# First attention: V of a group projected beside its own pairs, two places for transposed x, weight units by halves of the columns

## What is computed

```python
Q = jnp.einsum('bqd,hde->bqhe', x, W_Q) + b_Q
K = jnp.einsum('bkd,hde->bkhe', x, W_K) + b_K
V = jnp.einsum('bkd,hde->bkhe', x, W_V) + b_V
scores = jnp.einsum('bqhe,bkhe->bhqk', Q, K) / np.sqrt(d_head)
A = jax.nn.softmax(jnp.where(causal, IGNORE, scores), axis=-1)
z = jnp.einsum('bhqk,bkhe->bqhe', A, V)
x = _layernorm(x + jnp.einsum('bqhe,hed->bqd', z, W_O) + b_O)
```

## Time and profile before

| | us |
|---|---|
| median of three executions | 1614.74 |
| their spread | 1612.95 to 1619.67 |
| the profiled execution, its time | 1618.39 |
| its span, first to last instruction | 1616.6 |
| PE busy in the span | 1541.5 (95%) |
| DVE busy | 998.3 (62%) |
| ACT busy | 687.4 (43%) |
| POOL busy | 187.6 (12%) |

### The profile page before, as it was taken

One profiled execution on the slowest core, in us unless ns is written; L12 is line 12 of the kernel. 1 busy time (PEld: TensorE's weight loads), 2 busy tenths in 40 slices (PEclk: granted clock), 3 DMA queues, 4 the chain that ended last, 5 costly groups with the idle time before them and its releaser, 6 DMA issues.

```text
span 1616.6 us, 28670 instructions
## 1 busy us (share of the span) xinstructions
PE 1541.5 (95%) x11112; PEld 1330.8 (82%) x11112; DVE 998.3 (62%) x2113; ACT 687.4 (43%) x1809; POOL 187.6 (12%) x207
## 2 busy tenths in 40 slices
PE   6999999899999999989999899999989899999997
PEld 5888888689899999978888677777767798989896
DVE  6777776845454545575666567788864554444446
ACT  0544544622222222212233277788873344444443
POOL 1222222310000000020000114122210000000001
PEclk9999999999999999989999999999998899999999
DMA  6000100001010101100000376678740000000101
GB/s 209 2 15 1 41 2 1 27 25 40 22 43 27 50 26 38 32 1 33 1 33 1 44 124 86 87 100 135 95 66 27 1 26 27 27 26 14 38 0 52
DMA packets 43065, 66.51 MB, mean 41 GB/s; under 512 B 4560, under 2 KB 33488, under 8 KB 42832
## 3 DMA queue, kind: packets, MB, share of 16 engines
q1 hardware_dynamic: 42960, 65.09, 19.9%
HBM read 36.24 MB, written 2.10 MB: 24 GB/s over the span
## 4 chain that ended last, share of the span: by engine, by line
PE 86%; DVE 8%; DMA 2%; issue 2%; ACT 2%; SPq 1%; POOL 1%; DVEq 0%; POOLq 0%; ACTq 0%
PE ps L83 22%; PE ps L84 21%; PE ps L85 21%; PE ps L1617 3%; PE ps L1631 2%; PE ps L370 2%; PE ps L394 2%; PE ps L1662 2%; PE ps L1607 2%; PE ps L381 2%; PE ps L1645 1%; DMA nQs<-nQc_h 1%; PE ps L364 1%; PE ps L1604 1%; SPq L1459 1%
## 5 line engine op out<-in xcount | busy, mean ns | idle before, releaser
L880 DVE TENSOR_TENSOR m6hT_l<-m6h,m6hT_h 128x512 fp32r<-128x512 f32 x128 | 88.4, 692 | 185.5 <-ACT m6hT_h L785 185.4
L787 ACT ACTIVATE m2hT_h<-ps 128x512 fp32r<-128x512 f32 x128 | 76.4, 597 | 287.3 <-PE ps L85 287.3
L882 DVE SCALAR_TENSOR_TENSOR m2hT_l<-ps,m2hT_h 128x512 fp32r<-128x512 f32 x128 | 88.4, 691 | 162.0 <-ACT m2hT_h L787 161.9
L784 ACT ACTIVATE m6h<-ps,m6b 128x512 f32<-128x512 f32 x128 | 88.0, 688 | 216.2 <-PE ps L85 201.6
L1731 ACT ACTIVATE nPr<-ps,negm 128x128 f32<-128x128 f32 x512 | 146.7, 383 | 23.3 <-DVE negm L1828 23.3
L83 PE MATMUL ps<-w_h,m6hT_h 128*128 128x256 f32 x512 | 145.3, 284 | 2.4 <-DVE X L918 1.8
L85 PE MATMUL ps<-w_h,m6hT_l 128*128 128x256 f32 x512 | 145.7, 285 | 0.0
L84 PE MATMUL ps<-w_l,m6hT_h 128*128 128x256 f32 x512 | 145.0, 283 | 0.0
L85 PE MATMUL ps<-m2w_h,m2hT_l 128*128 128x256 f32 x448 | 126.8, 283 | 0.0
L84 PE MATMUL ps<-m2w_l,m2hT_h 128*128 128x256 f32 x448 | 126.7, 283 | 0.0
L83 PE MATMUL ps<-m2w_h,m2hT_h 128*128 128x256 f32 x448 | 126.3, 282 | 0.0
(11 more groups left out here) (286 smaller groups left out, 4310.6 us busy)
## 6 DMA issues: line engine op xcount, KB each, us to landing
nKm<-nKc_h SPq DMA_DIRECT2D x64, 128.0 KB, 4.6
nQs<-nQc_h SPq DMA_DIRECT2D x64, 128.0 KB, 5.9
raw<-in_w_e1i SPq DMA_DIRECT2D x9, 512.0 KB, 3.3
raw<-in_w_e1o SPq DMA_DIRECT2D x9, 512.0 KB, 3.2
raw<-in_w_e6i SPq DMA_DIRECT2D x9, 512.0 KB, 3.3
raw<-in_w_e6o SPq DMA_DIRECT2D x9, 512.0 KB, 3.4
raw<-in_w_a SPq DMA_DIRECT2D x8, 512.0 KB, 4.4
nKm<-nKc_l SPq DMA_DIRECT2D x32, 128.0 KB, 5.4
```

Of the source, the lines that this page charges most:

```text
L784: nc.scalar.activation(c.h32[:, u % 2, :], ps[:, u % 2, :], ACT.Gelu, bias=bias)
L787: nc.scalar.activation(c.hT[0][:, ch, :], ps[:, u % 2, :], ACT.Relu).then_inc(c.s["hi_ready"], 1)
L880: last = nc.vector.tensor_tensor(c.hT[1][:, ch, :], c.h32[:, u % 2, :], c.hT[0][:, ch, :].bitcast(F32), ALU.subtract)
L882: last = nc.vector.scalar_tensor_tensor(c.hT[1][:, ch, :], ps[:, u % 2, :], 0.0, c.hT[0][:, ch, :].bitcast(F32), ALU.max, ALU.subtract)
```

## The change

V of a group is projected in the first two steps of its own pairs (V0 behind T0 and V1 behind T1 of step 4G, V2 and V3 in step 4G+1) and no longer before them. The places of the next group's fills move: x to step 4G, Q0 and Q1 to step 4G+1, Q2 and Q3 to 4G+2, K0 to K3 to 4G+3, K3 behind the values. The transposed x has two places, since V of a group still reads its own while that of the next is written. The weight units hold one half of the columns for both chunks, so the first two fills of Q need one unit. The high halves of units 1 to 5 are written by ACT, the low ones by DVE. DVE copies x low ahead of the low half of unit 0, and the wait for the row and V bias loads moves to K2's place. The constants of the mixtures move a little, the columns' load stands one place earlier, and the transposes of the mixture's x begin at step 30.

```diff
+    def w_of_step(p):
+
+        G, k = divmod(p, 4)
+        if G >= NGW:
+            return [[], [], [], []]
+        own, later = [("v", (G, j)) for j in range(4)], G + 1 < NGW
+        q, key = ([(kind, (G + 1, j)) for j in range(4)] if later else [] for kind in "qk")
+        return ([own[0:1], own[1:2], [("x", (G + 1, 0))] if later else [], []],
+                [own[2:3], own[3:4], q[0:1], q[1:2]],
+                [q[2:3], q[3:4], [], []],
+                [key[0:1], key[1:2], key[2:3], key[3:4]])[k]
+
+    def w_start():
+        return [("x", (0, 0))] + [(kind, (0, j)) for kind in "qk" for j in range(4)]
+
+    w_place = {f: F for F, f in enumerate(w_start() + [f for p in range(NP) for at in w_of_step(p) for f in at])}
...
-    def w_fills(G):
-        return [(kind, (G, j)) for kind in "qkv" for j in range(4)] + ([("x", (G + 1, 0))] if G + 1 < NGW else [])
-
-    def w_of_step(p):
-
-        G, k = divmod(p, 4)
-        return w_fills(G + 1)[3 * k:3 * k + (4 if k == 3 else 3)] if G + 1 < NGW else []
...
-    W_X_AT, W_U_AT, W_W_AT = 28, NP, (28, 30)
+    A1_BY_ACT = (1, 2, 3, 4, 5)
+    W_X_AT, W_U_AT, W_W_AT = 30, NP, (28, 30)
...
-            w, unit = (w_q, 2) if kind == "q" else (w_k, 4)
-            if G == 0 and j == 0:
-                pe.wait_ge(prep_done, U_A1 + unit)
+            w, unit = (w_q, 0) if kind == "q" else (w_k, 2)
+            xh, xl = W.XT[G % 2]
+            if G == 0 and j % 2 == 0:
+                pe.wait_ge(prep_done, U_A1 + (unit + 1 + j // 2))
...
-            if G == 0 and j == 0:
...
+            if G == 0 and b == 0:
+                pe.wait_ge(prep_done, U_A1 + (5 + half))
...
-                pe.wait_ge(consts_dve, 7)
+                pe.wait_ge(consts_dve, 2)
...
-        x_hi(1)
+        for k in A1_BY_ACT:
+            act.wait_ge(raw_loaded[k % 2], (U_A1 + (k - k % 2)) * 8 + 16)
+            nc.scalar.activation(wA1[0][:, k * RAW:(k + 1) * RAW], raw[k % 2][:, :], ACT.Identity).then_inc(split_act, 1)
...
+            if kind == "x":
+                split_first()
+                w_vector_start(v)
+            elif (kind, i) in extra:
...
+            sp.dma_start(cols[:, :], cols_in).then_inc(cols_loaded, 16)
             load_a1(1)
-            sp.dma_start(cols[:, :], cols_in).then_inc(small_loaded, 16)
...
-            split_a1(0)
-            split_a1(1)
-            v.wait_ge(small_loaded, 48)
-            w_vector_start(v)
...
+            def high_a1():
+
+                v.wait_ge(raw_loaded[0], 16)
+                nc.vector.tensor_scalar(wA1[0][:, 0:RAW], raw[0][:, :], 1.0, None, ALU.mult).then_inc(split_hi, 1)
+
+            def low_first():
+                v.wait_ge(split_hi, 1)
+                nc.vector.tensor_tensor(wA1[1][:, 0:RAW], raw[0][:, :], wA1[0][:, 0:RAW].bitcast(F32), ALU.subtract).then_inc(prep_done, 1)
+
+            def low_a1(k):
+
+                v.wait_ge(split_act, A1_BY_ACT.index(k) + 1)
+                v.sem_inc(split_hi, 1)
+                w = cut(wA1, k * RAW, RAW)
+                nc.vector.tensor_tensor(w[1], raw[k % 2][:, :], w[0].bitcast(F32), ALU.subtract).then_inc(prep_done, 1)
+
+            def last_low():
+                low_a1(5)
+                v.wait_ge(small_loaded, 32)
+
+            nc.vector.memset(mhalf[:, :], -0.5).then_inc(consts_dve, 1)
+            v.wait_ge(consts_pool, 7)
+            nc.vector.tensor_copy(identb[:, :], ident[:, :]).then_inc(consts_dve, 1)
             mix_vector_start(v, M2)
             m2 = mix_vector_parts(v, M2)
-            w_vector(v, link, {("q", (0, 0)): lambda: split_a1(2), ("q", (0, 1)): lambda: split_a1(3), ("q", (0, 2)): constants,
-                               ("q", (0, 3)): lambda: split_a1(4), ("k", (0, 0)): lambda: split_a1(5),
-                               ("k", (0, 2)): lambda: split_a1(6), ("v", (0, 0)): lambda: split_a1(7)}, M2, m2)
+            high_a1()
+            w_vector(v, link, lambda: (low_first(), low_a1(1)),
+                     {("q", (0, 0)): lambda: low_a1(2), ("q", (0, 2)): lambda: low_a1(3), ("q", (0, 3)): constants,
+                      ("k", (0, 1)): lambda: low_a1(4), ("k", (0, 2)): last_low,
+                      ("v", (0, 1)): lambda: split_a1(6), ("v", (0, 3)): lambda: split_a1(7)}, M2, m2)
...
+    def halved(c):
+        return c.reshape(128, 2, 2, 512).transpose(0, 2, 1, 3).reshape(128, -1)
...
-    x["w_a1"] = np.concatenate([chunked(heads(a[f"L0_attn_W_{n}"])) for n in "QKV"]
+    x["w_a1"] = np.concatenate([halved(chunked(heads(a[f"L0_attn_W_{n}"]))) for n in "QKV"]
```

More of the change, by code:

```diff
@@ L164, in program @@
     consts_dve = sem("consts_dve")
+    cols_loaded = sem("cols_loaded")
     small_loaded = sem("small_loaded")
@@ L170, in program @@
     split_hi = sem("split_hi")
+    split_act = sem("split_act")
     split_whole = sem("split_whole")
@@ L208, in program @@
     GW, WT, NGW, NP = 2, 2 * S, B // 2, 2 * B
-    WF = 13
     W = Stage()
@@ L219, in program @@
     w_slot(0)
-    W.XT = pair(m, "wXT", [P, DC, WT])
+    W.XT = [pair(m, "wXT0", [P, DC, WT]), None]
     W.V[0] = m.place("wV0", [P, GW, H, 64], F32)
@@ L232, in program @@
     W.bq8 = m.place("wbq8", [P, 8], F32)
+    W.XT[1] = pair(m, "wXT1", [P, DC, WT])
     W.s = signals("w", "g_full xt_hi g_evac bq_ready s_full s_max p_exp rec_done p_ready pt_full pt_ready z_full zt_hi zt_ready "
@@ L235, in program @@
     W.ctx_loaded = [sem("w_ctx_loaded0"), sem("w_ctx_loaded1")]
-    w_q, w_k, w_v = ([t[:, i * 2048:(i + 1) * 2048].rearrange("p (k n) -> p k n", k=DC) for t in wA1] for i in range(3))
+    w_q, w_k, w_v = ([t[:, i * 2048:(i + 1) * 2048].rearrange("p (h k n) -> p h k n", h=2, k=DC) for t in wA1] for i in range(3))
     w_o = [t[:, 3 * 2048:4 * 2048].rearrange("p (k n) -> p k n", k=8) for t in wA1]
@@ L239, in program, with w_fill @@
     G0 = 4
-    def w_fill(G, kind, j=0):
-        return WF * G + {"x": 0, "q": 1, "k": 5, "v": 9}[kind] + j
-    def w_fills(G):
-        return [(kind, (G, j)) for kind in "qkv" for j in range(4)] + ([("x", (G + 1, 0))] if G + 1 < NGW else [])
     def w_of_step(p):
         G, k = divmod(p, 4)
-        return w_fills(G + 1)[3 * k:3 * k + (4 if k == 3 else 3)] if G + 1 < NGW else []
+        if G >= NGW:
[9 more added lines that the diff above has]
+    w_place = {f: F for F, f in enumerate(w_start() + [f for p in range(NP) for at in w_of_step(p) for f in at])}
+    def w_fill(G, kind, j=0):
+        return w_place[kind, (G, j)]
     def w_pairs(*at):
@@ L328, in project @@
                 for i in range(DC):
-                    last = split3(nc, bank[:, c2 * WT:(c2 + 1) * WT], w[0][:, i, ch * P:(ch + 1) * P],
-                                  w[1][:, i, ch * P:(ch + 1) * P], W.XT[0][:, i, :], W.XT[1][:, i, :], i == 0, i == DC - 1)
+                    wh, wl = (t[:, ch // 4, i, ch % 4 * P:(ch % 4 + 1) * P] for t in w)
+                    last = split3(nc, bank[:, c2 * WT:(c2 + 1) * WT], wh, wl, xh[:, i, :], xl[:, i, :], i == 0, i == DC - 1)
             last.then_inc(s["g_full"], 1)
         def project_v(G, j):
-            if G == 0 and j == 0:
-                pe.wait_ge(prep_done, U_A1 + 6)
+            b, half = divmod(j, 2)
+            xh, xl = W.XT[G % 2]
+            if G == 0 and b == 0:
+                pe.wait_ge(prep_done, U_A1 + (5 + half))
             bank = g_fill(w_fill(G, "v", j))
-            b, half = divmod(j, 2)
-            cols_v = slice(half * GT, (half + 1) * GT)
             for i in range(DC):
-                last = split3(nc, bank, W.XT[0][:, i, b * S:(b + 1) * S], W.XT[1][:, i, b * S:(b + 1) * S],
-                              w_v[0][:, i, cols_v], w_v[1][:, i, cols_v], i == 0, i == DC - 1)
+                last = split3(nc, bank, xh[:, i, b * S:(b + 1) * S], xl[:, i, b * S:(b + 1) * S],
+                              w_v[0][:, half, i, :], w_v[1][:, half, i, :], i == 0, i == DC - 1)
             last.then_inc(s["g_full"], 1)
@@ L419, in w_tensor @@
                     transpose_p(2 * (p - 2) + half)
-                for kind, i in f[half:half + 1]:
+                for kind, i in f[half]:
                     fill(kind, i)
@@ L423, in w_tensor @@
                 out_project(b)
-            for kind, i in f[2:3]:
+            for kind, i in f[2]:
                 fill(kind, i)
@@ L427, in w_tensor @@
                 values(p - 2)
-            for kind, i in f[3:]:
+            for kind, i in f[3]:
                 fill(kind, i)
@@ L441, in x_hi @@
             act.wait_ge(s["g_full"], F + 1)
-            nc.scalar.activation(W.XT[0][:, :, :].rearrange("p a b -> p (a b)"), ps[:, WG0 + F % 2, :],
+            nc.scalar.activation(W.XT[G % 2][0][:, :, :].rearrange("p a b -> p (a b)"), ps[:, WG0 + F % 2, :],
                                  ACT.Identity).then_inc(s["xt_hi"], 1)
@@ L473, in w_scalar @@
                     exponentials(2 * p + half)
-            for kind, (G, j) in w_of_step(p):
+            for kind, (G, j) in w_of_step(p)[2]:
                 if kind == "x":
```

(13 more changed lines are left out.)

6 lines of the change are left out of this document (removed).

## The result

The changed kernel takes 1620.39 us (median of 8 runs, 1618.43 to 1623.77), the kernel before 1616.62 us on the same chip: a ratio of 1.003, interval 1.0018 to 1.0041. That is 3.8 us slower, clear of no change by the interval, though under the 0.5% that the forecast took as the least a measurement can tell; the forecast was 3.5 us slower. It started from a median of 1614.74 us for the kernel before, of three executions; eight give 1616.62. The profiled execution took 1620.44 us with a span of 1618.7, against 1618.39 and 1616.6.

A forecast was written before the change was run, and what follows sets the result against it. TensorE was taken as full from 37 to 292 us, VectorE's chain as the bound at the end. Pair 28 1.0 us later plus 2.5 at the end gave + 3.5 on 1614.74: 1618.2 us, range 1610.5 to 1624.

The forecast's parts named there:

- Pair 0: Start: scores of pair 0 begin at 24.4 us instead of 36.43; 5.7 us left after allowing for fills moved out.
- What is late next: First gates: VectorE stands 4 us for context and token loads; pair 2 starts at 42.9 us instead of 48.53.
- C: Start: time the first context and token loads land, taken as 32.4 us; most of pair 2's start is counted from it.
- The stall at the group boundary: Pairs 4, 8 to 28: scores wait for the evacuation of K3, 0.94 us each, seven times, 6.6 us lost.
- The rival that it costs nothing: Group boundaries: the wait is met or hidden, so 3.1 us faster than before, 1611.6 us; chance 12%.
- the slower rival: Odd steps: VectorE empties a bank too late for the fourth fill; 8.5 us slower, 1623.2 us; chance 13%.
- The rest of the dense part: Pair 2 to pair 28: same number of fills, spread more evenly, so 243.8 us as before, apart from the stall.
- Pair 28: End of the dense part: pair 28 starts at 293.3 us, 1.0 later than before, four V fills still to do.
- The end: Step 28 onward: 1.5 us for 5.8 us of V work and 1.0 for two moved transposes, + 2.5 us.
- The term that failed: Steps 30 and 31: VectorE comes 1.0 us late to the maxima of pair 30; 16.1 us instead of 15.55.
- the two transposes moved there: Behind step 33: two transposes of the mixture's x move to where TensorE has no gap, + 1.0 us.
- a term for the clock: Named outside the sum: new gaps could halve TensorE's speed at the start (about + 2 us), filled steps spare some at the end (- 1).

The follow-up runs named there:

- e1: The changed kernel with the scores of each pair waiting only for their own half of the K fills: 1613.64 us, ratio 0.9984 to the kernel before.
- e2: The changed kernel with the first context and token loads issued behind weight unit 3 instead of unit 7: 1617.29 us, ratio 1.0008 to the kernel before.
- e5: The changed kernel without the four V fills of the last group (steps 28 and 29): 1621.29 us, ratio 1.0037 to the kernel before.
- e6: The changed kernel without the four V fills of middle group 4 (steps 16 and 17): 1617.73 us, ratio 1.0024 to the kernel before.
- e7: e3 with the splits of weight units 6 and 7 moved later, behind Q1 and K0 of group 1: 1608.62 us, ratio 0.9964 to the kernel before.
- e3: The changed kernel with both the edits of e1 and e2: 1607.72 us, ratio 0.9943 to the kernel before.

## Why the prediction was right, step by step

The mechanism was as forecast: a gain at the start that the token load cuts short, and a stall at seven group boundaries that eats it. That the total is so close (3.5 forecast, 3.8 measured) is luck: pair 28 was 1.5 later than forecast and the end 1.3 shorter.

**Pair 0** came at 25.21, not 24.4. Two terms of the sum were small. The high half on ScalarE was taken as 0.9 from the line through two rows of other shapes; it takes 1.06 (row at 22.03). The narrower of the two rows reads a second operand, negm, which the other and this one do not, so the line mixed two kinds. The Trainium skill ("ScalarE: Activation LUTs", What ACT_TABLE_LOAD costs) had it at an estimated 1.04, and the row agrees with it. And unit 5 landed at 22.0, not 21.4. Neither counted in the end, since pair 0 was not what pair 2 waits for: e1 made it 1.65 earlier and pair 2 did not come earlier.

**What is late next** was the step on which most hung, and it held. VectorE stands 3.99 us (4 forecast) in front of the first gate; the load lands at 33.2 (C was 32.4), pair 2 comes 10.4 behind it (10.5 forecast, 0.3 of it for the second split), at 43.64. e2 confirms the cause by taking the wait away. The token load is issued at 25.89 and lands some 7 us later, behind other loads, as in the earlier trace rows. The estimated 2.6 us for a 256 KB load by the Trainium skill ("DMA: Bandwidth & Descriptors", Anatomy of one DMA) does not agree with this either; that section gives its figure for one DMA on the path of GpSimd, and these loads are issued by SyncE, several at a time.

**The stall at the group boundary**: seven times 0.79 shown and 0.94 lost, forecast 0.94. (The forecast's 0.04 from the matmul's end to the evacuation stands in no row that it names; K3's evacuation, at 294.02 behind a matmul that ends at 293.98, has it.) e1 removes it and gets back 6.62 of 6.6. The rival that it costs nothing (TensorE's queue holds work) is out, and so is the slower rival: no odd step has a wait for a bank, and the four steps of a group take 9.79, 9.44, 9.42 and 10.46 with the stall (9.2 to 10.2 forecast, the last a little over).

**The rest of the dense part** held an error of count. I said that it has the same number of fills in it. From pair 2 to 28, e1, which has no stall, takes 244.51 against 243.77 before. From the rows of the masks: the kernel before takes 38.0 us a group (64.77, 102.77, 140.78 and so on) and 37.46 for steps 24 to 27, which have no x fill; e1 takes 38.0 there. That one x fill is 0.54, which I had missed. The rest of the six groups is 0.45 longer in all, and steps 2 and 3, with one fill fewer, 0.25 shorter. The sum is + 0.7.

**Pair 28** is therefore 2.5 late instead of 1.0 (294.77 against 292.30): 0.7 from pair 2, 0.7 from the count.

**The end** was forecast at + 2.5. From pair 28 to the marker it is 47.87 against 46.10 before, + 1.8. Step by step: step 28 takes 9.34 instead of 8.31 (9.2 forecast), step 29 takes 6.48 instead of 6.37 (6.45 forecast), step 30 takes 8.79 instead of 8.73 (9.3 forecast), and from pair 31 to the marker it is 23.26 instead of 22.69. So the V fills did cost what I had for their own two steps, + 1.1. The term that failed is the one behind them: VectorE was to come late to the maxima of pair 30, for 0.55 over steps 30 and 31, and step 30 shows 0.06. I also left out that the fills lie over waits (e5, and e6 for a middle group).

The + 0.6 behind pair 31 is speed. The values behind 2.13 us of idle time take 1.93 in the change (324.23); before:

```profile
320.56 1.13 PE L394 MATMUL ps<-wPT,wV 128*64 128x128 f32 x16 [2.13 <-ACT wPT L456]
```

But I cannot call that an effect of the change. From these values to the next ones the work is the same in all runs, and it takes 7.55 before, 8.10 in the change, 7.59 in e6 and 9.05 in e5, as the slow matmuls fall.

Behind the marker 0.6 comes back: x of the mixture is transposed at 353.52, against 349.89 before, so + 3.63. I had + 1.0 for the two transposes moved there, and that was right: from the end of the output projection to that place it is 7.01 before and 7.91 in the change, + 0.9. The output projection itself, though, takes 4.48 before and 2.97 in the change, 1.5 less. The rows behind it, before and then after:

```profile
342.88 0.40 PE L83 MATMUL ps<-m2XT_h,m2w 128*128 128x512 f32 x1
```

```profile
345.61 0.60 PE L725 MATMUL ps<-ident,X 128*128 128x128 f32 x4
```

TensorE was at a lower granted clock there before, in 338.4 to 342.4 us at 0.57, and the change has it at 1.00 in 342.6 to 346.6. The windows of 337 to 344 us, TensorE alone, before and then after (the second holds only the first 1.4 us of that projection):

```profile
337.00:344.00 7.00, 5.60 (x29) 0.76 0.00 0
```

```profile
337.00:344.00 7.00, 4.44 (x37) 1.00 0.01 2
```

So the forecast lacked a term for the clock, which it had named only in one sentence of both signs, and most of why the end is 1.3 short of the forecast is this - 1.5. It is luck too: e7, with the transposes in the same places as the change, has that projection at a low clock again (0.61, 330.69 to 335.16), and e1 to e6 have it at 1.00. Together, start and count + 2.47, end + 1.16: the + 3.63.

Between 707 and 747 us, far behind the change, the profile of after gets another 2.6 us back (+ 3.64 at 707.17, + 1.03 at 746.45), where the routed feed-forward part starts. There the kernel before waits 2.12 us at 723.47 and then runs 3.7 us at half speed, and the changed one does neither, behind a longer stretch at half speed ahead of that. The spans end 2.1 apart, the medians 3.8. I take this for a difference of two executions; what causes it stays open.

## What to carry to other kernels

When work is moved, look at what now stands last before the next user: a fill whose evacuation was covered by another fill costs the whole round trip (0.94 us, seven times) when nothing lies between, though the amount of work is nearly the same. Then ask whether the wait is as narrow as the data: here a pair needs half of K, and one changed wait gave 6.7 us back. An earlier start is worth only what the next late thing allows, so the loads of what comes next have to be moved along with it; the two mends together turned 3.8 us slower into 8.7 us faster.

## What the runs showed of the hardware

In a stretch that has idle time, taking matmuls away can gain nothing: leaving out 5.8 us of them in steps 28 and 29 (e5) made these steps 1.7 us shorter and changed nothing at the marker, since the granted clock of 292 to 323 us was 0.94 instead of 1.00 and that of a later output projection 0.63 instead of 1.00. Whether the second follows from the first is not shown.

After an idle time of 2.13 us the same 16 matmuls took 1.93 us in the change, 1.67 in e1 and 1.98 in e3 (2.14 idle), where the kernel before did them in 1.13 behind an idle time of the same 2.13 (at 320.56), and e5 and e7 in 1.09. The runs that began at full speed lost it later: the kernel before at the four transposes right behind (1.12 us, elsewhere 0.66), e5 and e7 in the output projection behind the next idle time, of 1.94 us. So where the half speed falls differs from run to run (each of another kernel), and with it the time of the same work, from these 16 matmuls to the next 16: 7.55 to 9.05 us.
